# Prelu in the result, the last chunk of the first layer in four PSUM banks, and GpSimd lining up the first load

## The reference, cut to what matters

```
x = x + L0(gn(x))   # y = gelu(x*w1); z = gelu(y @ wg); sum over 4 "m" of z*w2
x = x + L1(gn(x))   # depthwise 4x4 filter
x = x + L2(gn(x))   # attention within 8x8 windows
x = x + L3(gn(x))   # 3x3 involution with scattered sums, then batch norm:
                    #   yn = (yout - mean) * rsqrt(var + eps) * gamma + beta
                    #   where(yn >= 0, yn, 0.3 * yn)
```

## Time and profile before

| | |
|---|---|
| median of 3 runs | 1075.73 us (1072.3 to 1078.36) |
| profiled execution | 1075.53 us, its span 1072.9 us |
| TensorE / VectorE / ScalarE / GpSimd busy in the span | 73% / 65% / 52% / 30% |
| mean granted TensorE clock | 0.82 of 2.4 GHz |
| first load, to the end of the aggregation | 0 to 38.9 us |
| first layer, set 0 and set 1 | 41.2 to 184.6 us, and ends at 635.7 us |
| result | 945 us to the end |

### The profile page before, as it was taken

The page is one execution under the profiler, slowest core; times in us unless marked ns, Lnnn a source line. Parts: engine busy times, 40 slices in busy tenths (PEclk is TensorE's granted clock), DMA queues, the critical chain, the costliest instruction groups (busy, mean ns, idle before and its releaser), DMA issues. The chain is left out here.

```text
span 1072.9 us, 28694 instructions
## 1 busy us (share of the span) xinstructions
PE 783.7 (73%) x12508; PEld 564.6 (53%) x12508; DVE 701.1 (65%) x1085; ACT 560.3 (52%) x581; POOL 325.0 (30%) x265
## 2 busy tenths in 40 slices
PE   5589986897998547844888759979975487346664
PEld 4344442897887437511334319969854384024443
DVE  6556665997555993592223359965459925979993
ACT  4899992342444206357899913424442072525553
POOL 1111111740003880060000026200048700636665
PEclk8899997898999767855799969989986587557776
DMA  9322220000000000000000000000000000003556
GB/s 300 113 64 68 61 71 2 1 2 2 4 4 4 1 1 20 2 0 1 2 2 2 2 1 1 2 2 4 4 4 1 1 20 1 0 1 118 156 157 196
DMA packets 59932, 37.54 MB, mean 35 GB/s; under 512 B 1952, under 2 KB 59424, under 8 KB 59808
## 3 DMA queue, kind: packets, MB, share of 16 engines
q1 hardware_dynamic: 59808, 35.71, 11.0%
HBM read 18.93 MB, written 16.78 MB: 33 GB/s over the span
## 5 line engine op out<-in xcount | busy, mean ns | idle before, releaser
L376 PE MATMUL ps<-work,w2d 32*32 32x512 f32 x2048 | 155.1, 649 | 22.5 <-ACT work L636 15.7
L624 ACT ACTIVATE work<-X,l0s 128x2048 f32<-128x2048 f32 x64 | 133.5, 2089 | 5.1 <-SPq L320 3.8
L363 PE MATMUL ps<-work,cst 32*32 32x512 f32 x2048 | 100.8, 654 | 40.5 <-ACT work L636 21.6
L636 ACT ACTIVATE work<-ps 128x2048 f32<-128x2048 f32 x64 | 119.9, 1873 | 19.3 <-PE ps L363 19.3
L773 DVE SCALAR_TENSOR_TENSOR X<-ps,X 128x1024 f32<-128x1024 f32 x32 | 39.2, 1225 | 136.0 <-PE ps L376 136.0
L1099 POOL TENSOR_TENSOR work<-cst,work 128x512 f32<-128x512 f32 x64 | 69.6, 1109 | 178.7 <-SPq L320 158.0
L376 PEld LDWEIGHTS ps<-work,w2d 32*32 32x32 f32 x2048 | 63.1, 110 | 88.5 <-issue 75.4
L653 ACT ACTIVATE work<-ps 128x512 f32<-128x512 f32 x80 | 47.8, 597 | 110.6 <-PE ps L430 110.6
L441 PE MATMUL ps<-cst,work 128*128 128x143 f32 x640 | 95.2, 294 | 0.2 <-DVE X L823 0.2
L870 DVE TENSOR_TENSOR work<-ps,cst 128x512 f32<-128x512 f32 x64 | 44.3, 692 | 70.7 <-PE ps L477 70.7
L276 PE MATMUL ps<-ST,work 32*128 32x512 f32 x256 | 58.6, 1007 | 43.6 <-DVE work L1005 18.7
(11 more groups left out here) (105 smaller groups left out, 1557.2 us busy)
## 6 DMA issues: line engine op xcount, KB each, us to landing
out<-work SPq DMA_DIRECT2D x64, 256.0 KB, 3.2
work<-x SPq DMA_DIRECT2D x16, 512.0 KB, 5.2
work<-x SPq DMA_DIRECT2D x32, 256.0 KB, 2.9
work<-choose SPq DMA_DIRECT2D x8, 128.0 KB, 2.7
cst<-consts SPq DMA_DIRECT2D x1, 1009.5 KB, 9.5
cst<-consts SPq DMA_DIRECT2D x1, 64.0 KB, 1.9
```

Of the source, the lines that this page charges most:

```text
L363: last = pe.matmul(ps[C * k4:C * k4 + C, g, :], wg[rows, m, C * g:C * g + C], yb[rows, m % 2, k4 * BANK:(k4 + 1) * BANK], start=True, stop ...
L376: last = pe.matmul(ps[C * g:C * g + C, 4 + b, :], diag[rows, m, :], zb[rows, k % ZDEEP, g, :], start=(m == 0), stop=(m == MULTI - 1))
L624: act.activation(yb[:, k % 2, :], X[:, s * PIX + i * CHUNK:s * PIX + (i + 1) * CHUNK], ACT.Gelu, scale=l0s[:, at:at + 1], bias=l0s[:, at + ...
L636: act.activation(zb[:, (s * UNITS + k) % ZDEEP, :, :], ps[:, 0:4, :], ACT.Gelu).then_inc(s_zs, 1)
```

## The change

1. **Result.** ScalarE's `norm` uses Prelu with the slope 0.3 where it used Identity, and VectorE's `leaky` goes. GpSimd adds x to blocks 0 and 1 in one instruction and to block 2 in another; VectorE adds it to block 3 (`add_last`). `s_fl` goes, and GpSimd waits for ScalarE (`s_fy`).
2. **First layer, last chunk.** Half 1 is summed in banks 6 and 7, beside half 0, and each of its weighings stands right behind that of half 0. So that banks 6 and 7 are free, the 32 slices of the next set are spread over the first 28 steps (`NEXT`; the steps 0, 7, 14 and 21 take two). VectorE aggregates the next set's statistics ahead of the last two additions.
3. **First load.** GpSimd lines up the 16 slices; VectorE only measures. GpSimd's work on the constants comes behind the 16 slices.

```diff
-        def group_columns(s, j, b):
+        def group_columns(s, j, b, n):
...
+        NEXT = {}
+        for n in range(NB):
+            NEXT.setdefault(divmod(n * 28 // NB, MULTI), []).append(n)
...
@@ TensorE, weigh_z @@
-                    if m == 0 and 2 * n + hf:
+                    bank = 4
+                    if hf and i == PIX // CHUNK - 1:
+                        bank = 6
+                        if m == 0 and s + 1 < NS:
+                            pe.wait_ge(s_bank_b, NB)
+                    elif m == 0 and 2 * n + hf:
                         pe.wait_ge(s_x1, 2 * n + hf)
...
-                            last = pe.matmul(ps[C * g:C * g + C, 4 + b, :], diag[rows, m, :], zb[rows, k % ZDEEP, g, :],
+                            last = pe.matmul(ps[C * g:C * g + C, bank + b, :], diag[rows, m, :], zb[rows, k % ZDEEP, g, :],
...
@@ TensorE, the steps of chunk i @@
-                    weigh_z(i, 0, 0)
-                    weigh_z(i, 1, 0)
-                    next_set(4 * i + 2)
+                    for m in range(2):
+                        weigh_z(i, m, 0)
+                        if last_one:
+                            weigh_z(i, m, 1)
+                    next_sets(i, 2)
                     project_y(i, 3)
                     weigh_z(i, 2, 0)
-                    next_set(4 * i + 3)
-                    if i + 1 < PIX // CHUNK:
+                    if last_one:
+                        weigh_z(i, 2, 1)
+                    next_sets(i, 3)
+                    if not last_one:
                         project_y(i + 1, 0)
                     weigh_z(i, 3, 0)
-                for m in range(MULTI):
-                    weigh_z(PIX // CHUNK - 1, m, 1)
+                weigh_z(PIX // CHUNK - 1, 3, 1)
...
@@ TensorE, out_transposed @@
+                    if b == 3:
+                        pe.wait_ge(s_fd, q + 1)
...
@@ ScalarE, norm @@
-                act.activation(y, y, ACT.Identity, scale=bns[:, 12 + s:13 + s], bias=bns[:, 15:16]
+                act.activation(y, y, ACT.Prelu, scale=bns[:, 12 + s:13 + s], bias=bns[:, 15:16], alpha=LEAKY
...
@@ VectorE, first load @@
-                    dve.wait_ge(s_load[u], i * 16 + 16)
-                    dve.wait_ge(s_in, i * 8 + (2 * u + 2))
-                    dve.tensor_copy(lined[:, u % 2, :, :, :],
-                                    stage[:, u, :, :].rearrange("p g (w c) -> p w g c", c=C)).then_inc(s_lined, 1)
-                    if u:
-                        measure(i, u - 1)
-                measure(i, LOADS - 1)
+                    measure(i, u)
...
@@ VectorE, result @@
-            def leaky(q):
+            def add_last(q):
+                s, j = divmod(q, GROUPS)
                 dve.wait_ge(s_fy, q + 1)
-                y = row[:, q % OUT_ROWS, :, :].rearrange("p b n -> p (b n)")
-                dve.scalar_tensor_tensor(y, y, LEAKY, y, ALU.mult, ALU.max).then_inc(s_fl, 1)
+                y = row[:, q % OUT_ROWS, 3, :]
+                x_in = X[:, s * PIX + (3 * (W // 4) + TILES * j) * H:s * PIX + (3 * (W // 4) + TILES * (j + 1)) * H]
+                dve.scalar_tensor_tensor(y, y, 1.0, x_in, ALU.mult, ALU.add).then_inc(s_fd, 1)
...
@@ GpSimd, first load @@
+            for i in range(0, 4):
+                for u in range(LOADS):
+                    pool.wait_ge(s_load[u], i * 16 + 16)
+                    pool.wait_ge(s_in, i * 8 + (2 * u + 2))
+                    pool.tensor_copy(lined[:, u % 2, :, :, :],
+                                     stage[:, u, :, :].rearrange("p g (w c) -> p w g c", c=C)).then_inc(s_lined, 1)
             pool.wait_ge(s_const, 16)
...
@@ GpSimd, result @@
-                pool.wait_ge(s_fl, q + 1)
-                for b in range(0, 4, 2):
-                    y = row[:, q % OUT_ROWS, b:b + 2, :]
-                    pool.tensor_tensor(y, group_columns(s, j, b), y, ALU.add).then_inc(s_fo, 1)
+                pool.wait_ge(s_fy, q + 1)
+                for b, n in ((0, 2), (2, 1)):
+                    y = row[:, q % OUT_ROWS, b:b + n, :]
+                    pool.tensor_tensor(y, group_columns(s, j, b, n), y, ALU.add).then_inc(s_fo, 1)
```

More of the change, by code:

```diff
@@ L120, in columns @@
             return X5[:, ds(s * 4, 4), ds(w, 1), :].rearrange("p b o h -> p (b o) h")
-        def group_columns(s, j, b):
-            return X[:, s * PIX:(s + 1) * PIX].rearrange("p (b n) -> p b n", b=4)[:, b:b + 2, TILES * j * H:TILES * (j + 1) * H]
+        def group_columns(s, j, b, n):
+            return X[:, s * PIX:(s + 1) * PIX].rearrange("p (b n) -> p b n", b=4)[:, b:b + n, TILES * j * H:TILES * (j + 1) * H]
         def rows4(v):
@@ L247, in build @@
         s_fy = sem("out_y_ready")
-        s_fl = sem("out_l_ready")
-        s_fo = sem("out_half_sum_ready")
+        s_fd = sem("out_last_block_sum_ready")
+        s_fo = sem("out_block_sums_ready")
         s_ft = sem("out_transposed")
@@ L389, in next_set, with next_sets @@
                         last.then_inc(s_in_b, 1)
+                def next_sets(i, m):
+                    for n in NEXT.get((i, m), ()):
+                        next_set(n)
                 project_y(0, 0)
                 for i in range(PIX // CHUNK):
-                    next_set(4 * i)
+                    last_one = i == PIX // CHUNK - 1
+                    next_sets(i, 0)
                     if i:
@@ L772, in add_half @@
                     dve.wait_ge(s_acc, n + 1)
-                    dve.scalar_tensor_tensor(X[:, at:at + 2 * BANK], ps[:, 4:6, :].rearrange("p a b -> p (a b)"), 1.0,
+                    bank = 6 if hf and i == PIX // CHUNK - 1 else 4
+                    dve.scalar_tensor_tensor(X[:, at:at + 2 * BANK], ps[:, bank:bank + 2, :].rearrange("p a b -> p (a b)"), 1.0,
                                              X[:, at:at + 2 * BANK], ALU.mult, ALU.add).then_inc(s_x1, 1)
@@ L788, in _ @@
                 for i in range(PIX // CHUNK):
-                    store_next(4 * i)
-                    if i:
-                        add_half(i - 1, 1)
-                    store_next(4 * i + 1)
-                    store_next(4 * i + 2)
-                    store_next(4 * i + 3)
+                    for m in range(MULTI):
+                        for n in NEXT.get((i, m), ()):
+                            store_next(n)
+                        if i and m == 0:
+                            add_half(i - 1, 1)
+                    if s + 1 < NS and i == PIX // CHUNK - 1:
+                        dve.drain()
+                        dve.bn_aggr(mv_b[:, :], stats_b[:, :]).then_inc(s_aggr_b, 1)
                     add_half(i, 0)
-                if s + 1 < NS:
-                    dve.drain()
-                    dve.bn_aggr(mv_b[:, :], stats_b[:, :]).then_inc(s_aggr_b, 1)
                 add_half(PIX // CHUNK - 1, 1)
@@ L1016, in _ @@
                 if q:
-                    leaky(q - 1)
-            leaky(NS * GROUPS - 1)
+                    add_last(q - 1)
+            add_last(NS * GROUPS - 1)
         @block.gpsimd
@@ L1024, in _ @@
             pool.memset(warm[:, :], 0.0).then_inc(s_warm, 1)
-            pool.wait_ge(s_const, 16)
-            for m in range(MULTI):
-                last = pool.tensor_scalar(diag[:, m, :], c("mean8")[:, 0:C], c("w2")[:, m:m + 1], float(B),
-                                          ALU.mult, ALU.mult)
-            last.then_inc(s_diag, 1)
-            pool.tensor_tensor(c("wk"), c("wk"), c("temp"), ALU.mult)
-            pool.tensor_tensor(c("bk"), c("bk"), c("temp"), ALU.mult)
-            pool.tensor_tensor(c("bkc"), c("bkc"), c("tempc"), ALU.mult)
             cnt = [0]
@@ L1053, in first_scales @@
                      pool.tensor_tensor(l0s[:, at + MULTI:at + 2 * MULTI], c("w1"), nmr.broadcast_to([P, MULTI]), ALU.mult))
+            for i in range(0, 4):
[4 more added lines that the diff above has]
+                                     stage[:, u, :, :].rearrange("p g (w c) -> p w g c", c=C)).then_inc(s_lined, 1)
+            pool.wait_ge(s_const, 16)
+            for m in range(MULTI):
+                last = pool.tensor_scalar(diag[:, m, :], c("mean8")[:, 0:C], c("w2")[:, m:m + 1], float(B),
+                                          ALU.mult, ALU.mult)
+            last.then_inc(s_diag, 1)
+            pool.tensor_tensor(c("wk"), c("wk"), c("temp"), ALU.mult)
+            pool.tensor_tensor(c("bk"), c("bk"), c("temp"), ALU.mult)
+            pool.tensor_tensor(c("bkc"), c("bkc"), c("tempc"), ALU.mult)
             pool.wait_ge(s_aggr, 1)
```

2 lines of the change are left out of this document (1 added, 1 removed).

## The result

| | before | changed |
|---|---|---|
| median, us | 1076.53 (4 runs, 1072.3 to 1078.36) | 1030.93 (4 runs, 1027.11 to 1038.1) |
| ratio | | 0.959 [0.9524, 0.9655] |
| profiled execution, us | 1075.5 | 1038.1 |
| its span, us; granted clock | 1072.9 | 1036.3; 0.834 |

The changed kernel is faster, by 45.6 us of the median. The profiled execution of it is the longest of its four, so the trace shows 37.4 of them. Both views are needed: the trace says where time went in this one execution, the spread of the others (1027 to 1038) says that something in it varies. Medians are over all runs, ratios over the fast ones alone, so a ratio is not exactly the quotient of the medians beside it.

A forecast was written before the change was run, and what follows sets the result against it. The prediction took GpSimd's 4.66 us plus leaky's 2.17 us to set the result's period. Gains of 28.4 + 4.1 + 5.3 + 5.4 + 4.0 = 47.2 us from 1075.5 gave 1028 us, range 1016 to 1044.

The forecast's parts named there:

- The loop that bounds the result: Result: norm, lay, second half of the transposes, spread, scaled take 9.04 us for two groups at full clock.
- the steps of parts 2 and 3: First layer's last chunk: gains of 5.3 us in set 0, 5.4 in set 1; first load: 4.0 us.
- the likeliest case: Whole kernel: 1028 us, with 4.7 us a group in the result; chance 0.65, including stores that bound.
- rival A: Result: TensorE's clock stays low or toggles, period 5.4 to 5.8 us, total 1039 us; chance 0.22.
- the predicted range: Result, VectorE's add_last: between 0.6 and 2.9 us by what it waits for.
- Rival D: Result: Prelu makes ScalarE the bound, about 1080 us, milder form 1050 us; chance 0.03.
- Its first term: Tail behind scaled(15): norm(15) and lay(12) take 4.1 us before four groups are stored.
- a pair of halves: First layer's last chunk: weighings of both halves run side by side in about 1.15 us, bound 2.1 us.
- the early aggregation: First layer's end: the next set's aggregation, 1.02 us, stands in VectorE's wait for the last half 0, costing nothing.
- the double slices: Set 0's first layer: two slices in steps 0, 7, 14, 21; the last two delay ScalarE, together 1.1 us.
- In set 1 the term: First layer, set 1: the new last chunk gains 5.4 us.
- The mis-sized term: First load: 2.33 MB left at 23 us, at 326 GB/s 7.1 us, so the last slice lands at 30.1.

The follow-up runs named there:

- part 1 alone: The kernel before with only the result's edits (Prelu, add_last, GpSimd adding three blocks of four): 1048.28 us, ratio 0.9743.
- the additions on GpSimd: The changed kernel without add_last, GpSimd adding x to all four blocks: 1034.36 us, ratio 0.9595.
- the kernel again: The changed kernel measured and profiled a second time with no edit: 1037.16 us, ratio 0.960.
- with the filler: The changed kernel plus 72 needless TensorE transposes in set 1's first layer: 1028.54 us, ratio 0.9566.
- with the constants late: The changed kernel with the second DMA of constants behind the 16 slices and GpSimd's work on them later: 1028.31 us, ratio 0.957.
- with lay ahead: The changed kernel with lay(q-3) ahead of norm(q) on ScalarE: 1023.46 us, ratio 0.9512.

## Why the prediction was right

**The total.** 1028 us were forecast, 1030.93 measured, inside 1016 to 1044. The loop that bounds the result and the steps of parts 2 and 3 were right. The total owes something to luck: the two profiled executions saved 36.6 and 38.0 us of span where 47.2 were forecast, and the kernel's median was 1030.93 us in one measurement and 1037.16 in the other. What was missed is the clock outside the result, the tail, and 3.8 us lost in the other layers.

**Part 1.** The loop was named and sized ahead: 9.04 us for two groups, and the trace has 4.35 and 4.68 us in turn, 9.03. The forecast of 4.7 was this with a sixth of the groups at half clock. In the first profile none was (gain 30.5 us instead of 28.4); in the second the period was 5.3 on average from 969 us on (gain 22.9). So the likeliest case and rival A are both real, and a single execution takes one of them or a mixture. The weight of A, 0.22, looks too small, and it was drawn from one stretch that ran at 0.90 with TensorE 69% busy; the same instructions then ran at 1.00 and at 0.84. Of the six profiles in which ScalarE does norm ahead of lay, three toggled (part 1 alone, the additions on GpSimd, the kernel again) and three did not (the first, with the filler, with the constants late). Prelu costs 2.096 us (2.09 was taken), add_last 0.69 to 1.77 us in the predicted range. Rival D is out: the trace has two table loads, at 9.14 and 35.21 us, and none in the result, where norm and lay follow each other at 2.10 and 1.91 us. The Trainium skill ("ScalarE: Activation LUTs", Table sets: the hidden batching unit) names relu, copy, identity and abs as in every set and leaves Prelu unnamed; read as the prediction read it, it would have put a switch around each Prelu, and the trace disagrees.

**The tail** was sized 19.4 us and took 20.7 in both profiles. In the first of them the DMA moved 253 GB/s through it, 5.2 MB; the prediction counted 4.19 MB at 303 GB/s, and so took a higher rate and a group less. Its first term, norm(15) and then lay(12), is real: with lay ahead the tail is 3.6 us shorter. Why the DMA share is 0.85 and not 1 is not settled.

**Part 2.** The steps at the end were found: a pair of halves in 1.15 us (1.15), the last addition 3.8 us behind the last z (4.0), the early aggregation in a wait. What the double slices cost (1.1) no run takes apart. The gain in set 0 is 5.4 us (5.3) in these two profiles, which is close by luck: the three profiles without part 2 have 145.78 to 150.85 us for that layer, the nine with it 139.58 to 145.15. In set 1 the term was 5.4, and the profiles gave -1.5 and 7.3: the step at the end is the same to 0.1 us in both sets (z ends at 622.7, aggregation at 629.23: 6.5 us), the difference goes with the clock in the 100 us ahead of it (0.89 and 0.95). The 148.42 us of the first profile stand alone: the three profiles without part 2 have 145.74 to 148.08 us in set 1, the six others with part 2 and no filler 137.16 to 141.27. By the means (146.9 and, over all seven, 141.2 us) part 2 brings 5.8 us there. The variation was missed: the prediction weighed the clock for the result only, though this stage had 0.92 in the same window before.

**Part 3.** 3.2 us instead of 4.0. The copy was cheaper (1.04 instead of 1.15), but GpSimd had the last slice more than a us later than 30.1. The mis-sized term is the transfer. Until 23 us the DMA moved 316 GB/s instead of 326, so 2.55 MB were left instead of 2.33; the last bytes moved shortly before 31 us, and the copy began at 31.48. The rate did not fall behind 23 us: the 255 of the second window holds about 2 us with nothing left to move, and 23 to 29 us ran at 337. The windows of the changed kernel:

```profile
1.00:23.00 22.00, 13.13 (x72) 12.06 (x72) 11.08 (x17) 10.28 (x17) 10.11 (x11) 0.92 0.98 316
23.00:33.00 10.00, 6.98 (x52) 5.56 (x53) 8.44 (x14) 7.82 (x14) 6.87 (x9) 1.00 0.79 255
23.00:29.00 6.00, 4.10 (x32) 3.39 (x32) 4.81 (x9) 4.70 (x9) 3.89 (x5) 1.00 1.04 337
```

GpSimd's constants ended at 35.1, ahead of the aggregation's end at 35.67, and cost nothing.

**Not foreseen and open.** The second layer of set 0 takes 70.99 to 71.09 us in every profile with part 3 and 70.20 or 70.21 in every one without it (0.3 us more in set 1). The instructions of that layer are the same, and no run here takes it apart. The rest of the 3.8 us is scattered over stages whose clock differs from execution to execution.

## What to carry to other kernels

When an engine's stall is taken out, write down the next loop instruction by instruction with its order on every engine: that gave the period to 0.01 us, and the order on ScalarE then turned out to be worth 0.5 us a group, and 3.6 us in the tail, for no added work. Where a stage is bound by another engine and TensorE has short gaps, its clock can fall in some executions and make TensorE the bound: look at the granted clock of each stage in more than one profile before putting a gain or a loss down to an edit, and try work that does nothing in those gaps. Judge an edit of a few us in the stage it touches, since the total may hide it, and in several profiles, since a stage can change by that much with no edit.

## What the runs showed of the hardware

- The same instructions had the granted clock at 1.00 in one execution and at 0.84 in another (result), 0.89 and 0.95 (set 1's first layer). Reordering ScalarE did not end this: with lay first the result had a stretch at 0.85 and one at 1.00.
- 72 useless transposes, which keep TensorE busy 10.5 us, made a stage 3.9 and 5.2 us shorter against a profile without them each time. The Trainium skill ("TensorE: Matmul & The Clock Gate", Part 4: PE-mode transpose) says that a transpose in TensorE's transpose mode doesn't count as TensorE being busy in the same way; here, in fp32, a stretch with them among other products ran at 1.00 where it had 0.95 without. The trace lists them as MATMUL and does not say whether they ran in that mode.
- Two weighings on different tiles of the array, 32 records, took 1.15 us, one of 16 records took 1.09.
- A GpSimd copy of 128x1024 fp32 takes 1.04 us (1036 to 1042 ns, 16 of them), also beside VectorE's statistics, which read PSUM.
- VectorE's addition of 128x512 takes 0.69 us at least and 1.77 us at most beside GpSimd's additions of up to 128x1024 (2.25 us at most with lay first).
